# A fused linear-attention and expert kernel: phi(K)^T x per batch in place of the value projection

## What is computed

```python
Q = feature(xn @ Wq.T + bq);  K = feature(xn @ Wk.T + bk);  V = xn @ Wv.T + bv      # feature(t) = elu(t) + 1
KV = einsum('bshd,bshe->bhde', K, V)                     # 16 heads of 16
Z = 1 / (einsum('bshd,bhd->bsh', Q, K.sum(axis=1)) + 1e-6)
attn = einsum('bshd,bhde,bsh->bshe', Q, KV, Z) @ Wo.T + bo
probs = softmax(xn @ gate_w)                             # 8 experts
g, m = top_k(probs over tokens, 256);  h = gelu(xn[m] @ w1) @ w2;  ffn = scatter_add(g * h)
out = x + attn + ffn
```

## Time and profile before

| what | value |
|---|---|
| median of the three timed runs | 1902.31 us |
| the profiled execution: its span, from first to last instruction | 1898.3 us |
| median less span | 4.0 us |
| stage A: first projection to first expert matmul | 20.0 to 543.4 us |
| granted clock of TensorE, mean over the span | 0.998 |

### The profile page before, as it was taken

One profiled execution on the slowest core, in us unless ns is written; L12 is line 12 of the kernel. 1 busy time (PEld: TensorE's weight loads), 2 busy tenths in 40 slices (PEclk: granted clock), 3 DMA queues, 4 the chain that ended last, 5 costly groups with the idle time before them and its releaser, 6 DMA issues. The chain is left out here.

```text
span 1898.3 us, 38991 instructions
## 1 busy us (share of the span) xinstructions
PE 1863.2 (98%) x13562; PEld 1269.6 (67%) x13562; DVE 1300.6 (69%) x2611; ACT 1272.2 (67%) x2045; POOL 1026.2 (54%) x947
## 2 busy tenths in 40 slices
PE   6899999999999999999999999999999999999998
PEld 4566666666676666666666666666666666666666
DVE  6678999998857777655787875555555555555556
ACT  6988887777746666666666666666666666666664
POOL 5656565656445555654455455545554554555453
PEclk9999999999999999999999999999999999999999
DMA  6979897989675555666677667576766766676857
GB/s 174 231 221 247 216 251 240 225 236 254 190 191 132 122 120 123 148 179 150 165 157 181 154 158 183 135 177 151 192 152 160 169 143 180 155 187 154 183 120 223
DMA packets 448900, 338.22 MB, mean 178 GB/s; under 512 B 224757, under 2 KB 430330, under 8 KB 448762
## 3 DMA queue, kind: packets, MB, share of 16 engines
q1 hardware_dynamic: 383674, 253.84, 48.5%
q0 software_dynamic: 48864, 66.88, 19.8%
q10 hardware_dynamic: 16224, 15.73, 2.5%
HBM read 185.61 MB, written 100.40 MB: 151 GB/s over the span
## 5 line engine op out<-in xcount | busy, mean ns | idle before, releaser
L1961 PE MATMUL pY<-w2s,hid 128*128 128x256 f16 x6144 | 756.6, 273 | 0.8 <-DVE hid L1806 0.8
L1946 PE MATMUL pH<-xgT,w1s 128*128 128x512 f16 (+1 forms) x3120 | 747.7, 376 | 1.3 <-PEq L324 1.3
L1961 PEld LDWEIGHTS pY<-w2s,hid 128*128 128x128 f16 x6144 | 599.8, 98 | 180.6 <-DVE yo L1822 3.6
L1806 DVE SCALAR_TENSOR_TENSOR hid<-gel,cur,hid 128x512 f16<-128x512 f32 (+1 forms) x520 | 384.6, 740 | 446.4 <-ACT hid L1745 440.8
L1720 POOL DMA_INDIRECT acc<-yo,idx x254 | 405.9, 1598 | 523.0 <-DVE yo L1822 450.0
L1742 ACT ACTIVATE gel<-pH,cur 128x512 f32<-128x512 f32 (+1 forms) x520 | 353.8, 680 | 476.7 <-PE pH L1946 457.2
L1946 PEld LDWEIGHTS pH<-xgT,w1s 128*128 128x128 f16 x3120 | 305.1, 98 | 252.4 <-DMA xgT<-xg 1.6
L1745 ACT ACTIVATE hid<-gel,cur 128x512 f16<-128x512 f32 (+1 forms) x520 | 372.0, 715 | 17.1
L219 POOL DMA_INDIRECT xg<-table,idx x256 | 286.1, 1118 | 112.1 <-issue 58.2
L1270 PE MATMUL pP<-wkv,xT 128*128 128x512 f16 x768 | 201.8, 381 | 7.8 <-DVE bias_rows L981 4.7
L724 POOL TENSOR_SCALAR xm<-xring,moments 128x256 f32<-128x256 f32 x128 | 120.9, 954 | 72.3 <-DVE xhl L1002 72.2
(11 more groups left out here) (236 smaller groups left out, 1888.5 us busy)
## 6 DMA issues: line engine op xcount, KB each, us to landing
stage<-in_w SPq DMA_DIRECT2D x160, 512.0 KB, 6.4
xring<-in_x SPq DMA_DIRECT2D x16, 1024.0 KB, 6.4
x2ring<-in_x SPq DMA_DIRECT2D x16, 1024.0 KB, 7.6
table<-xhl SPq DMA_DIRECT2D x32, 512.0 KB, 4.1
mix<-x2ring SPq DMA_DIRECT2D x32, 512.0 KB, 3.0
acc<-zeros SPq DMA_DIRECT2D x16, 1024.0 KB, 4.6
fmix<-mix SPq DMA_DIRECT2D x48, 256.0 KB, 3.5
facc<-acc SPq DMA_DIRECT2D x48, 256.0 KB, 4.0
```

The source lines that it names most:

```text
L1806: v.scalar_tensor_tensor(out=hid[:, hc % 4, 1, w], in0=gel[:, hc % 2, w], scalar=cur[expert_of(b, q)][:, 1:2], in1=hid[:, hc % 4, 0, w], o ...
L1946: last = t.matmul(pH[hc % 4][:, tok], w[:, aw, c, hc * P:(hc + 1) * P], xgT[i][:, ad, c, tok], start=k == 0 and c == 0, stop=k == 2 and c ...
L1961: last = t.matmul(pY[s // 2][:, s % 2, :], hid[:, hc % 4, ad, s * P:(s + 1) * P], w[:, aw, hc, :], start=hc == 0 and k == 0 and s % 2 == 0 ...
```

## The change

V is no longer made. Since KV = K^T (xn Wv^T + bv) = (K^T xn) Wv^T + (sum of K) bv, the kernel adds up phi(K)^T xn over the tokens of a batch (the bank `pKV`, all 256 x 256 of it), and once per batch multiplies by Wv (`fold_v`), masks the heads (`blocks_out`), multiplies by Wo and adds the bias term as a rank-one update (`folded_out`). The left operand of the sum is the token-major pair of halves `xhl` that the transposes start from, so phi(K) has to be in halves too: ScalarE copies the high half out of `phik` (`key_high`), VectorE subtracts for the low one (`key_low`). The gate logits become 16 more columns of the key projection (`wkg`, 272 columns), and pass through the same VectorE instruction as the keys; `gate` and bank `pG` are gone, and bank `pS` takes the sum of phi(K), by four matmuls of one column. `blocks_out` and `folded_out` move from ScalarE to VectorE. GpSimd loses the bias and mask of the KV sums, keeps the two small `ksz` instructions, and does its four `add_bo` one by one between tiles. The last two tiles' sums of a batch are added in the next batch's body.

```diff
             def keys(n, j):
                 act.wait_ge(proj, at(proj, n, j))
                 act.wait_ge(k_done, at(k_done, n, j - 2))
-                    a.activation(ek[:, j % 2, :], pP[j % 2][:, 0:D], ACT.Relu, scale=winv_neg[:, 2:3]).then_inc(kneg_done, 1)
-                    act.wait_ge(kv_used, at(kv_used, n, j - 4))
-                    a.activation(kv1[:, j % 4, :, 0:P], pP[j % 2][:, :].rearrange("p (c t) -> p c t", c=2 * DC),
-                                 ACT.Copy, scale=winv[:, 2:3]).then_inc(kv_done, 1)
+                    a.activation(ek[:, j % 2, 0:D], pP[j % 2][:, 0:D], ACT.Relu, scale=winv_neg[:, 2:3], bias=1.0).then_inc(kneg_done, 1)
                     act.wait_ge(kneg_done, at(kneg_done, n, j))
+                    a.activation(ek[:, j % 2, 0:D], ek[:, j % 2, 0:D], ACT.Exp, scale=-1.0, bias=kln[:, 0:1]).then_inc(ek_done, 1)
+
+                def key_high(n, j):
+                    act.wait_ge(k_done, at(k_done, n, j))
+                    act.wait_ge(kv_used, at(kv_used, n, j - 4))
+                    a.activation(phk[:, j % 4, 0, :], phik[:, j % 4, 0:D], ACT.Copy).then_inc(khi_done, 1)
...
                 def k_feature(n, j):
-                    dve.wait_ge(kv_done, at(kv_done, n, j))
-                    dve.wait_ge(kv_used, at(kv_used, n, j - 4))
+                    dve.wait_ge(klo_done, at(klo_done, n, j - 4))
                     dve.wait_ge(ek_done, at(ek_done, n, j))
-                    v.scalar_tensor_tensor(
-                        out=phik[:, j % 4, :].rearrange("p (c t) -> p c t", c=DC), in0=kv1[:, j % 4, 0:DC, 0:P], scalar=0.0,
-                        in1=ek[:, j % 2, :].rearrange("p (c t) -> p c t", c=DC), op0=ALU.max, op1=ALU.add).then_inc(k_done, 1)
+                    v.scalar_tensor_tensor(out=phik[:, j % 4, :], in0=pP[j % 2][:, 0:GATED], scalar=KUNIT, in1=ek[:, j % 2, :],
+                                           op0=ALU.mult, op1=ALU.max).then_inc(k_done, 1)
+
+                def key_low(n, j):
+                    dve.wait_ge(khi_done, at(khi_done, n, j))
+                    v.tensor_tensor(phk[:, j % 4, 1, :], phik[:, j % 4, 0:D], phk[:, j % 4, 0, :], ALU.subtract).then_inc(klo_done, 1)
+
+                def blocks_out(m, alone=False):
+                    dve.wait_ge(kv_turned, at(kv_turned, m))
+                    v.tensor_tensor(kvT[:, :, :], bank_kv(m, alone)[:, 0:DC * P].rearrange("p (c t) -> p c t", c=DC),
+                                    head_mask[:, :].unsqueeze(1).to_broadcast([P, DC, P]), ALU.mult).then_inc(kvT_done, 1)
+
+                def folded_out(m, alone=False):
+                    dve.wait_ge(mo_mm, at(mo_mm, m))
+                    for c in range(DC):
+                        last = v.scalar_tensor_tensor(out=mo_of(m)[:, c, :], in0=bvo[:, c, :], scalar=ksring[:, m % 2, c:c + 1],
+                                                      in1=banks_mo[not alone][:, c * D:(c + 1) * D], op0=ALU.mult, op1=ALU.add)
+                    last.then_inc(mo_done, 1)
...
                 def project(n, j):
...
-                    pe.wait_ge(kv_done, at(kv_done, n, j - 2))
+                    pe.wait_ge(k_done, at(k_done, n, j - 2))
-                    terms = [(0, 0), (0, 1), (1, 0)]
-                    for k, (a, b) in enumerate(terms):
-                        for c in range(DC):
-                            last = t.matmul(pP[j % 2][:, :], xT[h][:, a, c, cols], wkv[:, b, c, :], start=k == 0 and c == 0,
-                                            stop=k == 2 and c == DC - 1, skip_group_check=True)
+                    for c in range(DC):
+                        t.matmul(bank[:, 0:GATED], xT[h][:, 0, c, cols], wkg[:, c, :], start=c == 0, stop=False, skip_group_check=True)
+                    t.matmul(bank[:, 0:D], bias_lhs[:, :], bias_rows[:, :], start=False, stop=False, skip_group_check=True)
+                    for c in range(DC):
+                        t.matmul(bank[:, 0:D], xT[h][:, 0, c, cols], wk_low[:, c, :], start=False, stop=False, skip_group_check=True)
+                    for c in range(DC):
+                        last = t.matmul(bank[:, 0:D + E], xT[h][:, 1, c, cols], wkg[:, c, 0:D + E], start=False, stop=c == DC - 1,
+                                        skip_group_check=True)
...
                 def sum_kv(n, j):
-                    pe.wait_ge(k_done, at(k_done, n, j))
-                    pe.wait_ge(kv_done, at(kv_done, n, j))
+                    pe.wait_ge(klo_done, at(klo_done, n, j))
...
                     for c in range(DC):
-                        last = t.matmul(pKV[:, c * (P + 1):(c + 1) * (P + 1)], phik[:, j % 4, c * P:(c + 1) * P],
-                                        kv1[:, j % 4, DC + c, :], start=j == 0 and c == 0, stop=j == NT - 1,
-                                        skip_group_check=True)
+                        for b in range(2):
+                            t.matmul(pS[:, c:c + 1], phk[:, j % 4, b, c * P:(c + 1) * P], one_col[:, 0:1],
+                                     start=j == 0 and c == 0 and b == 0, stop=j == NT - 1 and b == 1, skip_group_check=True)
+                    for k, (a, b) in enumerate(((0, 0), (0, 1), (1, 0))):
+                        for c in range(DC):
+                            last = t.matmul(pKV[:, c * D:(c + 1) * D], xhl[h][:, jj, a, c, :], phk[:, j % 4, b, :],
+                                            start=j == 0 and k == 0 and c == 0, stop=j == NT - 1 and k == 2, skip_group_check=True)
...
-                def turn_kv(m, alone=False):
-                        last = t.transpose(bank_kv(m, alone)[:, c * P:(c + 1) * P], kvm[:, c, :], ident[:, :])
+                def fold_v(m, alone=False):
+                    for c in range(DC):
+                        for cc in range(DC):
+                            last = t.matmul(bank_kv(m, alone)[:, c * P:(c + 1) * P], wvT[:, cc, c * P:(c + 1) * P],
+                                            gring[:, m % 2, cc, c * P:(c + 1) * P], start=cc == 0, stop=cc == DC - 1)
...
                 for n in range(NB):
...
+                        if n >= LAG and j in (1, 2, 5, 6):
+                            add_bo(n - LAG, (1, 2, 5, 6).index(j))
```

261 lines of the change are left out of this document (139 added, 122 removed).

## The result

The changed kernel takes **1927.16 us** (median of 4 runs, 1924.46 to 1929.55), the kernel before 1902.11 us beside it: a ratio of 1.0135 (95% interval 1.0121 to 1.0149), 1.35% slower. The forecast was 1909 us, so its sign is right and its size is not: +25 us in place of +6.6, and 1 us above the upper end of the range. The profiled execution is the shortest of the four, 1924.46 us with a span of 1922.7, 24.4 us more than the span of before.

The account below looks back on a forecast made before the run. The bound was to move from TensorE to VectorE. Terms 16.2 - 6.2 - 3.8 - 0.4 - 1.7 + 2.5 = +6.6 us on 1902.3 gave 1908.9, say 1909 us; range 1890 to 1926 us.

Parts of the forecast that it names:

- the change of the bound, and its price: Nine search batches: bound moves from TensorE to VectorE, 32.4 us plus 1.2 us waiting, period 33.6 us, +16.2 us in all.
- rival 4: VectorE's PSUM readers cost 0.065 us more each, 0.7 us a batch: 1915 us; chance 0.04.
- the collisions cost VectorE the same before and after: GpSimd against VectorE: spreading the four `add_bo` and removing masking work count as equal, leaving the sum alone.
- Rival 3: Search batches: single `add_bo` hold VectorE's two-input instructions, 2.7 us a batch, period 35.2 us, total 1924 us; chance 0.22.
- -2.0 and -1.8 us: Batches 0 and 1: gains taken from ScalarE's cheaper copies and TensorE's lighter tiles, -3.8 us in the sum.
- ScalarE's term: Batches 0 and 1: ScalarE loses a 687 ns copy per tile and gains a 256-element one, 8 x 0.27 = 2.1 us.
- the 29.1 of 33.6 us to come leave it at 2.4 GHz: TensorE's clock: busy 29.1 us of each 33.6 us period, it would stay at 2.4 GHz.
- -1.7: Batch 15: VectorE's 25.20 + 3.55 plus 0.9 us of waiting is 29.7 against 31.39 us, -1.7 us.
- batches 2 to 4, -6.2 us: Batches without a search: 29.5 us each against 31.43 and 31.88, -6.2 us together.
- TensorE's saving: TensorE per batch: 3.3 us less over eight tiles, +0.66 us for `fold_v`, so 2.6 us less, to about 29.1 us.
- the 29.5 us: Length of batches 2 to 4: VectorE 28.0 us, TensorE 28.3 to 29.3 us, with a little waiting 29.5 us.
- Tail, +2.5 us: End of the stage: `key_high` and `key_low` in a row, longer sum, two `fold_v` alone; +2.5 us, ends +1 and +4.

Follow-up runs that it names:

- no_low: Changed kernel with VectorE's eight `key_low` subtractions per batch left out, the low half of phi(K) being zero; 1897.38 us, ratio 0.9979 to before.
- no_bo: Changed kernel with GpSimd's four `add_bo` per batch left out, so the output lacks the output bias; 1909.02 us, ratio 1.0050 to before.
- before_extra: Kernel before the change with one more VectorE subtraction per tile where `key_low` would stand, nobody waiting for it; 1909.25 us, ratio 1.0047.
- no_bo_fold: Changed kernel without `add_bo`, and with both folding copies on ScalarE, without head mask and value-bias term; 1906.49 us, ratio 1.0034 to before.
- high_only: Changed kernel without the low half of phi(K): no `key_low`, none of TensorE's matmuls that use it; 1888.90 us, ratio 0.9932 to before.
- before_no_bo: Kernel before the change with GpSimd's `add_bo` left out, so its output lacks the output bias; 1900.46 us, ratio 0.9990.
- bvo_early: Changed kernel with `bias_blocks` moved to batch 0, tile 6 on VectorE and batch 1, tile 4 on TensorE, ScalarE's copy to tile 5; 1924.03 us.
- bvo_tail: Changed kernel with both `bias_blocks` moved as early and the last `key_low` ahead of the last batch's reciprocal; 1921.19 us, ratio 1.0100 to before.
- tail_low: Changed kernel with the last `key_low` issued ahead of the last batch's reciprocal, nothing left out; 1925.89 us, ratio 1.0135 to before.
- low_pool: Changed kernel with `key_low` moved from VectorE to GpSimd, nothing left out; 1952.59 us, ratio 1.0278 to before.
- fold_act: Changed kernel with `blocks_out` and `folded_out` on ScalarE as plain copies, head mask and value-bias term left out; 1929.21 us, ratio 1.0148 to before.

## Why the prediction was right or wrong

**Right: the change of the bound, and its price.** VectorE's batch was forecast at 32.4 us and is 32.2 (289.89 / 9); waiting at 1.2 us and is 1.6; the period at 33.6 and is 33.77. The nine batches were to cost 16.2 us and cost 17.6. `key_low` was taken at 0.45 us long and has 0.443, `k_feature` at 411 ns and has 418. no_low, no_bo and before_extra bear out the mechanism from both sides, with a limit: from 31.3 to 32.3 us of period on down the waits between the engines hold it, though neither VectorE nor TensorE is full (no_low, no_bo_fold, high_only). The PSUM surcharge (rival 4) is absent: `blocks_out`, which reads PSUM, has a mean of 418 ns, and before_extra's subtraction of the same width out of SBUF 416. `k_feature` hardly spreads, as foreseen: 410 to 441 ns.

**Right, but assumed: the collisions cost VectorE the same before and after.** They are 1.7 us a batch in the kernel before and 1.9 in the changed one (before_no_bo, no_bo); no row had shown that, and other instructions are met. Rival 3 priced them at 2.7: mostly two of four meet something, for 0.9 and 1.1 us, and where three do, for 2.6 us together, the batch is no longer. The total, 1927 us, lies beside rival 3's 1924, but its period of 35.2 us did not come: that is chance. What the prediction did not say is that the same lengthening, worth 1.5 us under TensorE's bound, is 18 us of the changed kernel's time.

**Where the miss lies.** The span grew by 24.3 us up to the first expert matmul where 6.6 were forecast. The 17.7 us between them are +8.3 in batches 0 and 1, -2.5 in the start, +3.9 in batches 2 to 4, +1.4 in the nine search batches, +0.3 in batch 14, +5.4 in batch 15 and +0.8 in the tail.

**Wrong: batches 0 and 1, "-2.0 and -1.8 us", for +4.5.** The start and batch 0 end together 1.2 us sooner than before (at 46.17 and 47.38 us), 0.8 less than forecast. The step that failed is in batch 1, 3.3 us longer for 1.8 shorter, and is what was not priced: `bias_blocks` stands in the diff between batch 1's first projection and the sums, and a new wait on TensorE has behind it everything that TensorE does. It cost 4.28 us of idle time and was followed by some 6 us at the low clock. bvo_early and bvo_tail have batch 1 at 28.7 and 29.1 us, so 3.7 to 4.2 us of the miss are this wait and what follows it. The window's low mean clock adds little: tail_low has the same wait, a mean of 0.92 in place of 0.81, and a batch 1 of 32.63 us in place of 32.85. The rest is ScalarE's term, "2.1 us". The copy does cost 0.3 us a tile less, but the exponential takes 508 ns where it took 448, the copies of the sums 0.92 us where they took 0.42, and the bias copy 0.58 is new: in bvo_early's batch 1 ScalarE is busy for 26.4 us where it was 27.3, and the batch, 29.6 us before, is shorter by the same 0.9.

**Wrong: "the 29.1 of 33.6 us to come leave it at 2.4 GHz".** It did so in the nine batches (1.00 in the window of all nine), but not in single stretches beside them: it fell in batch 1 after 4.28 us of idling, in batch 14 (mean 0.95, without a price: 32.53 us, and 32.52 in bvo_early at 1.00), and in batch 15:

```profile
517.20 1.73 DVE L1051 TENSOR_TENSOR qring<-qraw,eq 128x512 f32<-128x512 f32 x1 [0.38 <-ACT eq L832]
...
520.61 0.81 PE L1342 MATMUL pKV<-phk,xhl 128*128 128x256 f16 x6
522.74 3.41 PE L1407 MATMUL pO<-mo,qz 128*128 128x256 f32 x8 [1.32 <-issue]
...
527.01 1.89 PE L1407 MATMUL pE<-mo,qz 128*128 128x256 f32 x8
```

The four last `add_bo` run in one block from 515.87 us and lengthen `qring` to 1.73 us; TensorE waits 0.77 and 1.32 us, and its eight output matmuls take 3.41 us, 1.5 more than the next eight. Where `qring` got away with 0.91 us, in bvo_tail, batch 15 kept the clock and lasted 25.5 us. In tail_low the same block lengthened `qring` to 1.59 and `key_low` to 1.53 us, the clock stayed at 1.00, and batch 15 lasted 27.3. So about 2.5 of the 3.7 us in batch 15 are what this block happens to meet, with or without the clock, and 1.2 VectorE's added work, where -1.7 was forecast. Without any `add_bo` the batch lasts 24.66 us (no_bo) and 23.16 in before_no_bo, so the added work alone makes it longer, by 1.5.

**Wrong in size: batches 2 to 4, -6.2 us for -2.3.** TensorE's saving was summed to 2.6 us a batch; by the nine batches it is 2.0 (285.84 to 267.52 us busy, a ninth of it). Batches 2 and 3 have TensorE busy for 29.36 of 30.04 us; the 29.5 us were 0.5 too low. They do not follow TensorE alone: no_low, with the same matmuls, has batch 2 at 29.05 us. Batch 4 carries VectorE's first search work (1.4 us), has longer `key_low` and `qring` (means of 578 and 912 ns; 418 and 754 in batch 3), and lasts 31.67 us; the prediction had put it with 2 and 3.

**Tail, +2.5 us for +3.3.** Two us arise between the last `k_feature` and the first divide: `key_low`, `blocks_out` and `folded_out` on VectorE and 0.36 us of waiting for them. Moving `key_low` won back 0.8 there and 1.2 in the whole tail of tail_low's trace. The rest, 1.3 us, lies in the second pair of folding matmuls; that was only read from the trace, not taken out by a run.

What stays open: what makes `gsub` or the fourth `add_bo` go first, or moves the first `add_bo` by the 0.6 us that lie between batches 6 and 7, and why single batches (the seventh search batch in no_low, 34.46 us, and in bvo_early, 36.12) are longer at a mean clock of 0.95, while bvo_early's eighth has the same 0.95 and lasts 33.12.

## What to carry to other kernels

When a change moves the bound from one engine to another, price again what the old bound had covered: GpSimd's meetings with VectorE went from 1.5 us to 18 while they lengthened VectorE's work by about the same. A helper that is run once still needs a price if it waits: look at what is queued ahead of its producer and behind its consumer. A total that comes out as expected doesn't prove its parts: compare stretch by stretch, as no_low and bvo_tail show. Before moving work to a less busy engine, count the order in its queue and whom the moved instruction meets, not its share of busy time.

## What the runs showed of the hardware

- A VectorE instruction of 0.19 us is held by a GpSimd one with two SBUF inputs for up to its whole length (1.33 us beside 1.27); when both start within 0.01 us either may go first, and this decides between search batches of 33.1 and 33.9 us.
- The same 128 x 256 subtraction takes 417 ns on VectorE (no_bo) and 726 ns on GpSimd (low_pool, batch 7).
- TensorE fell from 2.4 to 1.2 GHz after pauses of 0.77 and 1.32 us (the row at 522.74 above), having worked without a pause before them; in tail_low it was busy for only 2.92 of 6 us at the same place and kept its clock. In fold_act six of the nine search batches have a mean clock of 0.95 and three of 1.00, and all but one last 34.0 to 34.2 us.
